# Two expert slots weighted and added on VectorE ahead of one down projection

## The reference

```
e = sel[:, k];  mask = one_hot(e, 8)
x1 = x @ W1.T + lora1(e);  x3 = x @ W3.T + lora3(e)
x2 = silu(x1) * x3                                  # 896 features
down = x2 @ W2.T                                    # W2: shared
a2 = gather(einsum('tf,erf->ter', x2, A2), e)       # 8 experts x rank 32
lora2 = einsum('ter,ehr->th', mask * a2, B2)
out = out + (down + lora2) * rw[:, k:k+1]
```

## Time and profile before

| | us |
|---|---|
| median of 3 runs | 1453.36 |
| profiled execution, its own time | 1458.43 |
| its span | 1456.6 |
| PE busy (matmul) | 1267.4 |
| DVE busy | 733.7 |
| ACT busy | 420.4 |
| POOL busy | 79.7 |

### The profile page before, as it was taken

How to read it: one execution, slowest core, us unless ns; L and a number is a source line. 1 busy time by engine, 2 the same in 40 slices (tenths; PEclk the granted TensorE clock), 3 DMA queues, 4 the chain that set the end, 5 groups by cost and what they waited for, 6 DMA issues and landing times.

```text
span 1456.6 us, 17482 instructions
## 1 busy us (share of the span) xinstructions
PE 1267.4 (87%) x6780; PEld 964.1 (66%) x6780; DVE 733.7 (50%) x1695; ACT 420.4 (29%) x909; POOL 79.7 (5%) x69
## 2 busy tenths in 40 slices
PE   5689998997998969888788899989989988798878
PEld 4468575765767859666556765747567667686656
DVE  4543278585446446334434233876944554553241
ACT  2523020221232432334443421212123323323341
POOL 0000000000110210000000000000001101100000
PEclk9999999898999989799987899999989999897989
DMA  9100000000000000000000000000000000000000
GB/s 365 44 1 0 0 1 1 0 1 0 1 1 1 1 1 1 1 0 8 1 8 1 0 1 1 1 0 1 0 1 1 1 0 1 1 1 1 0 1 15
DMA packets 3409, 16.98 MB, mean 12 GB/s; under 512 B 256, under 2 KB 2304, under 8 KB 2816
## 3 DMA queue, kind: packets, MB, share of 16 engines
q10 hardware_dynamic: 1152, 13.77, 2.3%
q1 hardware_dynamic: 2176, 2.10, 0.4%
HBM read 14.82 MB, written 1.05 MB: 11 GB/s over the span
## 4 chain that ended last, share of the span: by engine, by line
PE 62%; DVE 17%; ACT 9%; issue 8%; POOL 3%; DMA 1%; ACTq 0%; DVEq 0%; SPq 0%; POOLq 0%
PE bank L654 58%; ACT scr L1229 4%; DVE scr L1726 3%; DVE scr L1725 3%; PE bank L661 2%; POOL fac L2026 1%; DVE scr L1641 1%; ACT scr L1207 1%; PE bank L761 1%; ACT XnT L1207 1%; DVE negmax L1573 1%; DVE X L1483 1%; DVE scr L1498 1%; DVE XnT L1882 1%; POOL rstd L2026 1%
## 5 line engine op out<-in xcount | busy, mean ns | idle before, releaser
L654 PE MATMUL bank<-pack,scr 128*128 128x512 f32 (+2 forms) x944 | 330.0, 500 | 11.5 <-ACT scr L1207 10.0
L654 PE MATMUL bank<-XnT,pack 128*128 128x256 f32 x1024 | 272.4, 409 | 25.3 <-ACT XnT L1207 12.1
L654 PEld LDWEIGHTS bank<-pack,scr 128*128 128x128 f32 x944 | 183.0, 201 | 133.5 <-issue 101.1
L654 PEld LDWEIGHTS bank<-XnT,pack 128*128 128x128 f32 x1024 | 207.3, 207 | 67.1 <-ACT XnT L1207 14.8
L654 PE MATMUL bank<-scr,pack 128*128 128x256 f32 x944 | 239.0, 395 | 6.9 <-DVE scr L1641 6.6
L654 PEld LDWEIGHTS bank<-scr,pack 128*128 128x128 f32 x944 | 184.8, 198 | 39.3 <-DVE scr L1641 9.0
L1651 DVE TENSOR_TENSOR scr<-bank,scr 128x256 f32<-128x256 f32 x112 | 47.2, 424 | 150.4 <-ACT scr L1278 148.6
L1207 ACT ACTIVATE scr<-bank 128x512 f32<-128x512 f32 (+7 forms) x112 | 51.0, 472 | 241.4 <-PE bank L661 138.6
L1278 ACT ACTIVATE scr<-bank 128x256 f32<-128x256 f32 x112 | 42.5, 384 | 253.3 <-PE bank L654 251.9
L1229 ACT ACTIVATE scr<-bank,negmax 128x256 f32<-128x256 f32 (+1 forms) x256 | 82.9, 445 | 97.5 <-DVE negmax L1573 97.4
L1571 DVE TENSOR_REDUCE negmax<-bank 128x2 f32<-128x512 f32 x64 | 43.9, 686 | 97.3 <-PE bank L654 97.3
(11 more groups left out here) (175 smaller groups left out, 1424.5 us busy)
## 6 DMA issues: line engine op xcount, KB each, us to landing
pack<-pack_dram ACTq DMA_DIRECT2D x1, 6408.0 KB, 19.8
pack<-pack_dram ACTq DMA_DIRECT2D x1, 2052.0 KB, 30.6
pack<-pack_dram ACTq DMA_DIRECT2D x1, 1595.0 KB, 25.3
X<-x SPq DMA_DIRECT2D x4, 256.0 KB, 3.5
pack<-pack_dram ACTq DMA_DIRECT2D x1, 1024.0 KB, 21.9
out_dram<-X SPq DMA_DIRECT2D x4, 256.0 KB, 2.1
pack<-pack_dram ACTq DMA_DIRECT2D x1, 911.5 KB, 6.4
pack<-pack_dram ACTq DMA_DIRECT2D x1, 657.5 KB, 26.4
```

What stands on the lines that cost most here:

```text
L654: return pe.matmul(o, l, r, start=start, stop=stop, skip_group_check=True)
```

## The change

In the blocks with s % 2 == k (`joined`), which are (0,0), (1,1), (0,2) and (1,3):
- `gates` writes, after `rw`, four 128x128 diagonal tiles `rwd` (identity times the weight of a token, for two slots and two halves of the tokens). A new stage `rw_spread`, issued at the start of `experts`, multiplies a matrix of ones by them on PE (two matmuls of 256 columns), which leaves the weights of all tokens on every partition; ACT moves them to `rwb`.
- In `x_second`, VectorE multiplies the silu by slot 1's weight, then by x3, multiplies slot 0's x2T by slot 0's weight, and adds: x2T[1, m] becomes the weighted sum of both slots. These are four operations, each waiting for the one before, for one so far.
- `down` of slot 0 multiplies only the A2 half (256 columns); `down` of slot 1 multiplies all 512 by the sum. X is updated once, from slot 1's product, without a weight.
- The masks follow from this: for slot 0 the difference of the two one-hots times slot 0's weight, for slot 1 the bare one-hot.

`rwd` lies in the place of x2T[1, 5] and x2T[1, 6], which are written later, `rwb` in a part of aT that is no longer needed.

```diff
+        def joined(k, s):
+
+            return s % 2 == k
...
+            if joined(k, s):
+                stage("rw_spread", k, s)
             for m in range(FT + 2):
...
+            def rw_spread(k, s):
+                r = (k, s)
+                pe.wait_ge(rwd_ready[s], nth(s, 1, 1))
+                o = claim(pe, ("rwb", r))
+                for i in range(TOPK):
+                    last = mm(o[:, i * T:(i + 1) * T], w("ones"), rwd[s][:, i, :, :].rearrange("p a t -> p (a t)"), True)
+                last.then_inc(full[ring.bank(("rwb", r))], 1)
...
-                    last = mm(o[:, :], x2T[s][:, i, m, a * P:(a + 1) * P], wd[:, m, :], m == 0, m == FT - 1)
+                    c0 = D if i == 0 and joined(k, s) else 0
+                    last = mm(o[:, c0:2 * D], x2T[s][:, i, m, a * P:(a + 1) * P], wd[:, m, c0:2 * D],
+                              m == 0, m == FT - 1)
...
+            def rw_spread(k, s):
+                key = ("rwb", (k, s))
+                wait_full(act, key)
+                move(key, rwb[s][:, :, :], psum(key, 2, T))
...
+                if joined(k, s):
+                    for a in range(NT):
+                        for i in range(TOPK):
+                            ins = dve.tensor_scalar(rwd[s][:, i, a, :], ident, rw[s][:, i, a:a + 1], None, ALU.mult)
+                            if a * TOPK + i < NT * TOPK - 1:
+                                step(ins)
+                    ins.then_inc(rwd_ready[s], 1)
+                    link(dve.tensor_tensor(onehotw[s][:, :, 0, :], onehot[s][:, :, 0, :], onehot[s][:, :, 1, :],
+                                           ALU.subtract))
+                    for a in range(NT):
+                        step(dve.tensor_scalar(onehotw[s][:, a, 0, :], onehotw[s][:, a, 0, :], rw[s][:, 0, a:a + 1],
+                                               None, ALU.mult))
+                    step(dve.tensor_copy(onehotw[s][:, :, 1, :], onehot[s][:, :, 1, :]))
...
+                if m == 0:
+                    wait_drained(dve, ("rwb", r))
+                link(dve.tensor_tensor(act_out, act_out, rwb[s][:, 1, :], ALU.mult))
+                link(dve.tensor_tensor(x2T[s][:, 1, m, :], psum(key, 2, T)[:, 1, :], act_out, ALU.mult))
+                link(dve.tensor_tensor(act_out, x2T[s][:, 0, m, :], rwb[s][:, 0, :], ALU.mult))
+                dve.tensor_tensor(x2T[s][:, 1, m, :], x2T[s][:, 1, m, :], act_out, ALU.add).then_inc(drain_of(key), 1)
...
+                if not joined(k, s):
+                    link(dve.scalar_tensor_tensor(out=X[s][:, a, :], in0=o[:, 0, :],
+                                                  scalar=rw[s][:, i, a:a + 1], in1=X[s][:, a, :],
+                                                  op0=ALU.mult, op1=ALU.add))
+                elif i:
+                    link(dve.tensor_tensor(X[s][:, a, :], o[:, 0, :], X[s][:, a, :], ALU.add))
```

More of the change, by code:

```diff
@@ L194, in hybrid_kernel @@
             v, _ = part(s, 4 * T, [KER, T]); am2T.append(v)
+        rwd, rwb = [], []
+        for s in range(S):
+            rwb.append(part(s, 2 * T, [2, T])[0])
+            rwd.append(part(s, 4 * T + 2 * 4 * T + SX * T + (2 * FT - 2) * T, [2, NT, P])[0])
         lg = alternate(lambda s: sb(f"lg{s}", [P, NT, E]))
@@ L269, in hybrid_kernel @@
             v, o = part(s, 0, [HT1, T]); HT.append(v)
-        for held in (kT, vT, QT, KpT, latT, pvs, prob, probT, ctxn, ctxT, aT, amT, silu_x, x2T, am2, am2T, am2b, rot,
+        for held in (rwd, rwb, kT, vT, QT, KpT, latT, pvs, prob, probT, ctxn, ctxT, aT, amT, silu_x, x2T, am2, am2T, am2b, rot,
                      rtmp, bV, prod, sc, pw, convT, tokm, gate, kb, bv, KTt, QTt, KbT, QgT, PT, sqs, kd, kbg, qg, osq,
@@ L310, in hybrid_kernel @@
         am_ready = each("am_ready")
+        rwd_ready = each("rwd_ready")
         silu_ready = each("silu_ready")
@@ L1175, in ffn_half @@
                     last.then_inc(full[ring.bank(("fy", r))], 1)
[L1177 removed]
+            table = dict(rw_spread=rw_spread, delta_sq=nothing, consts=nothing, top_exp=nothing, ffn_half=ffn_half, delta_expand=nothing, delta_diag=nothing, conv_tap=nothing, gates=nothing, down_sum=down_sum, angles=nothing, norm_x=nothing, norm_t=norm_t, latent=latent, kv=kv, kv_fold=kv_fold,
                          scores=scores, weights=weights, values=values, values_t=values_t, out_in=out_in, out_proj=out_proj, router=router, spread_t=spread_t, spread=spread, x_first=x_first,
@@ L1626, in gates @@
                 link(dve.tensor_tensor(rw[s][:, 1, :], rw[s][:, 2, :], rw[s][:, 0, :], ALU.mult))
[L1627 to L1630, removed]
+                if joined(k, s):
[11 more added lines that the diff above has]
+                    step(dve.tensor_copy(onehotw[s][:, :, 1, :], onehot[s][:, :, 1, :]))
+                else:
+                    for a in range(NT):
+                        for i in range(TOPK):
+                            step(dve.tensor_scalar(onehotw[s][:, a, i, :], iota, topf[s][:, a, i:i + 1],
+                                                   rw[s][:, i, a:a + 1], ALU.is_equal, ALU.mult))
                 settle()
@@ L2002, in angles @@
                 ins.then_inc(trig_in, 1)
-            table = dict(delta_sq=delta_sq, consts=consts, top_exp=nothing, ffn_half=nothing, delta_expand=delta_expand, delta_diag=delta_diag, conv_tap=conv_tap, gates=gates, down_sum=nothing, angles=angles, norm_x=norm_x, norm_t=nothing, latent=latent, kv=kv, kv_fold=kv_fold,
+            table = dict(rw_spread=nothing, delta_sq=delta_sq, consts=consts, top_exp=nothing, ffn_half=nothing, delta_expand=delta_expand, delta_diag=delta_diag, conv_tap=conv_tap, gates=gates, down_sum=nothing, angles=angles, norm_x=norm_x, norm_t=nothing, latent=latent, kv=kv, kv_fold=kv_fold,
                          scores=scores, weights=weights, values=nothing, values_t=values_t, out_in=nothing, out_proj=out_proj, router=router, spread_t=nothing, spread=spread, x_first=x_first,
```

14 lines of the change are left out of this document (7 added, 7 removed).

## The result

| | before | after |
|---|---|---|
| median, us (4 runs each) | 1453.57 (1450.36 to 1456.19) | 1481.03 (1473.66 to 1488.99) |
| profiled execution, us | 1458.43 | 1475.27 |
| its span, us | 1456.6 | 1473.4 |
| granted clock, mean over the span | 0.927 | 0.917 |
| PE busy, us | 1267.4 | 1253.6 |

The change makes the kernel slower: the ratio of after to before is 1.0191 (95% interval 1.0122 to 1.026), 27.5 us between the medians and 16.8 us between the two profiled spans. The forecast was 1463 with a range up to 1473. The direction was right; the loss is three times what the sum gave.

What follows compares the result with a forecast made beforehand. PE was taken as the bound (87% busy, 62% of the chain of waits), block by block. (0,0) -2.6, (0,2) +2.1 and (1,1), (1,3) +5.0 each gave +9.5 on the median 1453.4, so 1463; range 1450 to 1473.

Steps and rivals of the forecast that it cites:

- Removed work: Slot 0's `down` stages in all four blocks: narrower records save PE 6.0 us a block, 24.1 us in four.
- the loss of cover before `delta_rows`: (1,1) and (1,3): shortening the slot 0 stage before L995 by 3.0 gives nothing; 3.0 of 6.0 us are left.
- The starts: Waiting for the diagonals, plus spread: 3.4 us in (0,0), 3.9 in (0,2), 3.5 each in (1,1) and (1,3).
- The three more operations: Each second product's chain ends 1.4 us later: twice each in (1,1) and (1,3), 4.2 us in all in (0,2).
- That becomes 1.4 longer: Second conv in (1,1) and (1,3): PE's 2.93 us wait for the second product of x(2) grows by 1.4.
- x(4)'s bank: PE's wait for the bank of x(4) in (1,1): forecast 0, later claims meeting the same predecessors.
- I count one of the two, 1.7 a block: (1,1) and (1,3): of two new idle stretches each, one is followed by the lower clock, costing 1.7 us.
- Case C: Clock falls at every new idle stretch, two each in (1,1), (1,3), one each in (0,0), (0,2): +16.3, 1470; chance 0.22.
- Case D: Linked operations pile up in other queues, up to three more chains a block: +26, 1480; chance 0.05.
- The bound given for the operations, 39 us: DVE's 28 longer chains: 0 if each is hidden behind PE's work, 39 us if none is.
- the bound of the clock, 3.5 us a block: (1,1) and (1,3): lower clock after new idle stretches, 1.7 a block counted, bounds 0 and 3.5.

Runs made afterwards that it cites:

- e1_narrow_only: Kernel after with only the narrow slot 0 stages and the dropped update of X kept, no spread or weighted sum: 1438.86 us, ratio 0.9888.
- e1_again: The same kernel as e1_narrow_only, in another group of runs: 1437.17 us, ratio 0.9851.
- e2_no_spread: Kernel after without the stage rw_spread and DVE's wait for it, so the weights are wrong: 1462.78 us, ratio 1.0069.
- e4_pool_later: Kernel after with GpSimd starting its two multiplies only after the product of x(2), in (1,1) and (1,3): 1468.81 us, ratio 1.0099.
- e13_k1_only: The change applied in (1,1) and (1,3) alone: 1482.71 us, ratio 1.0189 to the kernel before.
- e12: e1_narrow_only with the first slot 0 stage of (1,1) and (1,3) wide again (512 columns): 1435.43 us, ratio 0.9852.
- e3: Kernel after with one product instead of four linked operations, so the weighted sum is missing: 1462.22 us, ratio 1.0052.
- e10: Kernel after with the second product taken first from PSUM, freeing the bank, then weighting and adding: 1468.8 us, ratio 1.0075.
- e6: The change applied in (0,0) and (0,2) alone: 1452.56 us, ratio 0.9964 to the kernel before.
- e14_after_wide: Kernel after with the first slot 0 stage of (1,1) and (1,3) wide again, nothing else: 1470.38 us, ratio 1.0109.
- e7_ratio_k0: Ratio-of-weights form (two diagonals, one spread matmul, two added operations) in (0,0) and (0,2), rest as before: 1444.83 us, ratio 0.9937.

## Why the prediction was wrong

- Removed work, -24.1 us: the amount was right and so was the loss of cover before `delta_rows`. e1_narrow_only gave 15 us (1439 expected, 1438.86 measured), e1_again 20 against its own runs of before.
- The starts, 14.3 us: right within 0.4 in (0,0) and (1,1) (3.67 us idle for 3.7, 2.31 for 2.6, the diagonals 0.88 for 0.9). In (0,2) after's trace has 1.7 us for 3.9. e2_no_spread gave 18 us.
- The three more operations: right before `delta_rows` (+1.4; 5.07 for 5.1) and in (0,2) (5.28 and 2.09 for 5.3 and 2.1, and 1.00 for 1.4). At the second conv, "That becomes 1.4 longer" failed: the wait became 4.0 longer. The sentence priced operations with two SBUF inputs by L1651, whose operations read a PSUM bank, though the earlier trace rows shows POOL busy in that stretch. e4_pool_later shows the cause, GpSimd beside them: 3.4 us in each block. With x(4)'s bank, 2 x (2.56 + 0.58) = 6.3 us are missing in the sum for this.
- The clock: in "I count one of the two, 1.7 a block", 3.4 us in all, the size failed, and by the medians it is the larger part of the miss. Three readings give it. In the two profiled executions the clock costs 2 x 2.4 us inside (1,1) and (1,3), and PE's busy time has 6.8 us too much in all. In e13_k1_only, PE's busy time is 1267.1 us where the columns give 1267.4 - 12.1 + 1.8 = 1257.1: 10.0 us. And within one kernel, executions differ by the clock: in 64 runs of the kernel before, each about the mean of its group, time rises by 8.7 us for each 0.01 of mean granted clock less; in 96 runs of the others, each about its own kernel's mean, by 11.0. The median clock is 0.9135 in after's four runs and 0.930 in those 64 (of the four runs of before beside after no clocks are on record). By that slope, 0.0165 is an estimate of 14 to 18 of the 27.5 us.
- In the sum, 9.5 - 3.4 + 6.3 = 12.4 us stand without the clock, and with it 27 to 31, for a measured 27.5. For e13 alone it is 10.0 - 3.4 + 6.3 = 12.9, and with 0.013 of clock (0.931 to 0.918) 24 to 27, for a measured 27.5. This is an account that adds up, not a proof of each part: between two kernels the mean clock also falls by low stretches in which PE stands and which cost nothing.
- Why the size failed: I took the price from what follows one idle stretch, twelve records, at one place and in one execution. The granted clock fell over whole blocks (0.93 and 0.91 over 110 us), with four idle stretches in each where there had been two; and e12 and e1_again show that the same wait can cost 1.6 us or nothing. The two profiled executions, 16.8 us apart, are no fair picture of the medians, by luck: after's profiled execution has a clock of 0.917, its median is 0.9135. Case C, which pays for every new stretch at the same 1.7 us, was short as well (1470). Case D had nearly the right time (1480) for the wrong reason: apart from 0.6 us at x(4)'s bank, no wait for DVE's further chains shows in the blocks.
- That idleness brings the lower clock, and is not only found beside it, is seen at two places in the table of six kernels, one execution each; the wait of 2.94 us that cost nothing in e12 says that it is not so every time. How the rest of the clock's 14 to 18 us divides over the execution stays open, and so does how much the clock gives back in e2, e3, e4 and e10: each came out 2 to 7 us beyond the idle time taken out, but with after at 1.0152 instead of 1.0191, which e13 and e6 would make it, that excess is gone in most of them.
- The range ended at 1473 and left out case D. The bound given for the operations, 39 us, reached far beyond it, and the bound of the clock, 3.5 us a block, was itself too small by the medians.

## What to carry to other kernels

Before PE's work is traded for operations on another engine, ask of each stage that gets shorter what it was covering; then ask what the new idle time does to the clock of the whole stretch, and price that from runs of one kernel at different mean clocks, not from the few records behind one wait. Where the freed work only turns into a wait, leave it in: here the wide stage cost nothing in one kernel and gained 6 to 12 us in another. An operation moved to VectorE that reads two SBUF tiles has to be placed with GpSimd's queue beside it, and the one that frees a bank should read PSUM and come first.

## What the hardware showed that was not expected

- VectorE beside GpSimd: 128x256 operations of two SBUF tiles took 1.58, 1.11 and 1.99 us for 0.42, and the one with a PSUM input 0.42, in the same chain. GpSimd's two multiplies took 3.08 us in it for 2.90 before.
- 6 us of additional matmul columns made a kernel faster, by 12 us against after and by 6 us against the product of e13 and e6 (e14_after_wide, 1.0109 against 1.0191 and 1.0152).
- The same wait of 2.94 us was followed by twelve records in 4.47 us in one execution and in 2.86 in another (e1_again, e12_fill_gap).
- Executions of one kernel spread with the clock: after's four runs by 15.3 us (clock 0.905 to 0.919), e7_ratio_k0's ten by 17 us (0.920 to 0.936), and e14_after_wide's four, all at 0.921 or 0.922, by 3.6 us.
